# Attention outputs of two heads in one strip of a PSUM bank, and a phase's outputs turned by four transposes

## The reference

```python
x = x + L0_attn(layernorm(x))                # 16 heads of 8: causal, linear attention with elu + 1
x = x + L0_xattn(layernorm(x), ctx, mask)    # 16 heads of 8: 512 keys from ctx, masked softmax
x = x + L0_ffn(layernorm(x))                 # 8 experts, the best 2 of each token
x = x + L1_attn(layernorm(x))                # 16 heads of 8: 256 keys, a window of 128 back
x = x + L1_xattn(layernorm(x), ctx)          # 8 heads of 16: 512 keys, two softmaxes that share a sum,
                                             # then layernorm, relu ffn, layernorm
x = x + L1_ffn(layernorm(x))                 # ternary weights, gelu
# each softmax attention, per head:
attn = softmax(scores(q, k)); out = attn @ v
```

## Time and profile before

| | us |
|---|---|
| median of 3 runs | 1060.52 (1055.59 to 1060.76) |
| the profiled execution, whole | 1054.23 |
| its span, first to last instruction | 1052.5 |
| PE busy / weight loads busy | 848.7 / 475.7 |
| DVE / ACT / POOL busy | 666.6 / 488.6 / 321.2 |
| mean granted TensorE clock | 0.914 |

### The profile page before, as it was taken

How to read it: one execution, slowest core, us unless ns; L and a number is a source line. 1 busy time by engine, 2 the same in 40 slices (tenths; PEclk the granted TensorE clock), 3 DMA queues, 4 the chain that set the end, 5 groups by cost and what they waited for, 6 DMA issues and landing times.

```text
span 1052.5 us, 19620 instructions
## 1 busy us (share of the span) xinstructions
PE 848.7 (81%) x6455; PEld 475.7 (45%) x6522; DVE 666.6 (63%) x2234; ACT 488.6 (46%) x1017; POOL 321.2 (31%) x872
## 2 busy tenths in 40 slices
PE   0477786999999887989999877897999977866763
PEld 0344553443444543545555435674544444422452
DVE  6767556878777774777676757765678473533511
ACT  0432332655555553557666545365655625413331
POOL 6423333212132232224452224352421213320312
PEclk9788988999999998999999989799999998857875
DMA  6287876031230534345330447328140114233000
GB/s 193 60 157 158 179 175 132 20 54 30 42 69 5 107 92 84 71 81 106 52 83 26 66 89 155 54 95 127 34 71 4 48 21 84 74 64 63 2 6 5
DMA packets 124965, 79.85 MB, mean 76 GB/s; under 512 B 8312, under 2 KB 122176, under 8 KB 124736
## 3 DMA queue, kind: packets, MB, share of 16 engines
q1 hardware_dynamic: 124864, 78.59, 36.9%
HBM read 43.99 MB, written 32.90 MB: 73 GB/s over the span
## 4 chain that ended last, share of the span: by engine, by line
PE 45%; DVE 17%; DMA 13%; issue 7%; SPq 6%; POOL 6%; ACT 5%; DVEq 0%; another core or an unknown queue 0%; POOLq 0%; ACTq 0%
PE ob L1211 7%; PE mb L1153 6%; DMA cT<-ctxT_dram 5%; PE eb L1181 4%; PE side L1074 3%; PE eb L1182 3%; PE side L1082 3%; DMA bounce<-scratch 2%; DMA QW<-bounce 2%; PE side L1027 2%; DVE junk L1635 2%; PE side L1065 2%; PE side L1094 2%; DMA QP<-mrow 2%; DVE mx L1643 2%
## 5 line engine op out<-in xcount | busy, mean ns | idle before, releaser
L1365 ACT ACTIVATE probs<-eb 128x512 f32<-128x512 f32 (+1 forms) x512 | 274.8, 568 | 217.5 <-PE eb L1182 91.5
L1635 DVE CUSTOM_DVE_ANT_0 junk<-mb,maskq_add 128x512 bf16<-128x512 f32 x256 | 169.1, 688 | 49.0 <-PE mb L1153 37.4
L1211 PE MATMUL ob<-probs,V 128*32 128x256 f32 (+1 forms) x2048 | 133.3, 379 | 5.1 <-ACT probs L1365 2.2
L1643 DVE TENSOR_REDUCE mx<-mb 128x1 f32<-128x512 f32 x128 | 83.5, 685 | 56.1 <-PE mb L1153 53.7
L1181 PE MATMUL eb<-maskk_add,identb 128*128 128x512 bf16 x256 | 98.1, 383 | 9.7 <-issue 6.6
L964 POOL TENSOR_SCALAR nm<-mx 128x8 bf16<-128x8 f32 x80 | 20.1, 251 | 277.1 <-DVE mx L1635 117.9
L1153 PE MATMUL mb<-KS,QP 128*128 128x512 bf16 x227 | 81.3, 386 | 12.0 <-DVE mx L1635 6.9
L1182 PE MATMUL eb<-QP,KS 128*128 128x512 bf16 x231 | 88.3, 382 | 0.0
L1211 PEld LDWEIGHTS ob<-probs,V 128*32 128x32 f32 x2048 | 55.4, 111 | 65.6 <-issue 32.1
L874 POOL TENSOR_SCALAR rstd<-mv 128x2 f32<-128x2 f32 x64 | 16.5, 258 | 209.0 <-DVE mv L1431 207.8
L1374 ACT COPY OT<-ob 128x512 f32<-128x512 f32 x56 | 32.8, 585 | 73.4 <-PE ob L1205 44.0
(11 more groups left out here) (189 smaller groups left out, 1707.4 us busy)
## 6 DMA issues: line engine op xcount, KB each, us to landing
QP<-bounce SPq DMA_DIRECT2D x48, 256.0 KB, 5.5
KS<-bounce SPq DMA_DIRECT2D x32, 384.0 KB, 7.2
bounce<-scratch SPq DMA_DIRECT2D x48, 192.0 KB, 2.3
bounce<-scratch SPq DMA_DIRECT2D x64, 128.0 KB, 2.2
KS<-bounce SPq DMA_DIRECT2D x32, 192.0 KB, 6.0
bounce<-scratch SPq DMA_DIRECT2D x16, 384.0 KB, 2.6
cT<-ctxT_dram SPq DMA_DIRECT2D x16, 256.0 KB, 6.1
bounce<-scratch SPq DMA_DIRECT2D x16, 256.0 KB, 2.4
```

Of the source, the lines that this page charges most:

```text
L1211: ins = nc.tensor.matmul(bank[32 * j:32 * j + 32, S - n:S], v_of(core, kt, 4 * g + j), pr[:, (j % 2) * n:(j % 2 + 1) * n], start=(kt == 0) ...
L1365: nc.scalar.activation(probs[:, u % PROBS, 0:n], eb[:, u % 2, 0:n], ACT.Exp, scale=SCALE[core.p]).then_inc(probs_by[1], 1)
L1635: ins = V_.tensor_tensor_reduce(junk[:, e.n % 2, :], bank, maskq_add[:, t, :], 1.0, NEG_EXP, ALU.add, ALU.max, mx[slot][:, t, h:h + 1])
L1643: ins = V_.tensor_reduce(mx[slot][:, t, h:h + 1], bank, AX.X, ALU.max)
```

## The change

The values of heads 8 to 15 stand in columns 17 to 24 of their 32 and their 1.0 in column 25; heads 0 to 7 are as before. The group g + 2 adds its product onto the columns of group g in the same 256 columns of `ob`: only the first product of a strip clears, the last group ends the sum. All other columns of `V` are zero there, so the two heads don't mix. A phase now has one bank, one copy to `OT` (half as large as before) and one wait of the av; `outputs` turns all of `OT` by four 128x128 transposes and drops nothing, and `scaled` and `values` work on the lower and upper eight heads in an instruction each (two reciprocals and two products where one was). `v_of` also drops the tight packing of phase 3's values. In the planner `outputs` costs 0.65 instead of 1.8 (1.0 in phase 3), and a phase has one `keep`. Cut to its core:

```diff
@@ -40,7 +40,8 @@
-V_AT = (8, 8, 8, 0)
+
+V_AT = ((8, 17), (8, 17), (8, 17), (0,))
...
@@ -63,7 +64,7 @@
 
 
 def finish_steps(p):
-    return [("pe", "outputs", (1.8, 1.8, 1.8, 1.0)[p], ()), ("pool", "biased", 0.75, ()),
+    return [("pe", "outputs", 0.65, ()), ("pool", "biased", 0.75, ()),
             ("dve", "scaled", 0.95, ("outputs",)), ("pe", "scaled turned", 0.28, ("scaled",)), ("act", "scaled kept", 0.3, ("scaled turned",)),
             ("pe", "projected", 0.5, ("scaled kept",)), ("dve", "updated", 0.45, ("projected", "biased"))]
 
...
@@ -387,10 +387,9 @@
                 elif EXP_UNITS[core.p] * GROUPS[core.p] <= EARLY and exp_next == 1:
                     todo.append((CHAIN_OF[core.p + 1], core.b, t, core))
                 if u % QUAD == QUAD - 1:
-                    per = 2 * EXP_UNITS[core.p] // QUAD
                     a = Event("av", core, j // QUAD, 0, u // QUAD)
-                    a.first, a.last = a.g % per == 0, a.g % per == per - 1
-                    a.pair = sum(GROUPS[c.p] // 2 for c in exp_cores[:-1]) + a.g // per
+                    a.first, a.last = j == QUAD - 1, exp_next == EXP_UNITS[core.p] * GROUPS[core.p]
+                    a.turn = len(exp_cores) - 1
                     av_queue.append(a)
             elif kind == "exp":
                 ev = exp_queue.pop(0)
...
@@ -403,13 +402,12 @@
                 free[e] = t + AV_PE[ev.core.p]
                 av_done.append(free[e] + SEEN)
                 if ev.last:
-                    k = Event("keep", ev.core, ev.g // (2 * EXP_UNITS[ev.core.p] // QUAD), 0, ev.pair)
+                    k = Event("keep", ev.core, 0, 0, ev.turn)
                     k.made = free[e] + SEEN
                     keep_queue.append(k)
-                    if k.g == GROUPS[ev.core.p] // 2 - 1:
-                        slot_free[ev.core.slot] = free[e] + SEEN
-                        if ev.core.wide >= 0:
-                            wide_free[ev.core.wide] = free[e] + SEEN
+                    slot_free[ev.core.slot] = free[e] + SEEN
+                    if ev.core.wide >= 0:
+                        wide_free[ev.core.wide] = free[e] + SEEN
             elif kind == "keep":
                 ev = keep_queue.pop(0)
                 if ev.core.out < 0:
...
@@ -594,7 +590,7 @@
         nmr = sbs(SLOTS, "nmr", [P, TQ, 16])
         nm = sbs(SLOTS, "nm", [P, TQ, 16, PARTS], BF16)
         mrow = sbs(MROWS, "mrow", [MAX_ROWS, S], BF16)
-        OT = sbs(OUTS, "OT", [P, 4, S])
+        OT = sbs(OUTS, "OT", [P, 2, S])
         qn = sbs(QN, "qn", [P, TQ, D])
         cT = sbs(LANES, "cT", [P, SK])
 
...
@@ -972,7 +968,9 @@
                 for i in range(SLOTS):
                     yield 0.5 + 5 * i
                     link(G.memset(V[i][:], 0.0))
-                    G.memset(V[i][:, :, :, 16:17], 1.0).then_inc(values_init, 1)
+                    for j, at in enumerate(V_AT[0]):
+                        ins = G.memset(V[i][:, :, 8 * j:8 * j + 8, at + 8:at + 9], 1.0)
+                    ins.then_inc(values_init, 1)
 
             program("pool", {"nm": minus_maxima}, chain_steps, values())
 
...
@@ -1015,17 +1013,13 @@
             def finish(run, p):
                 l, o = run.lane, run.old.out
                 bank = side[:, l, :]
-                n, heads = HD[p] + 1, HEADS[p]
                 yield "outputs"
-                pe.wait_ge(out_kept, OB + PAIRS_TO[run.old])
+                pe.wait_ge(out_kept, OB + PHASES_TO[run.old])
                 if run.name in ("to1", "to3"):
                     pe.wait_ge(ctx_kept[l], N_CTX(run) + 1)
-                chosen = ident[:].rearrange("p (h e) -> p h e", e=VW)[:, :, V_AT[p]:V_AT[p] + n]
                 for t in range(TQ):
-                    for g in range(GROUPS[p]):
-                        lo = (t * heads + 4 * g) * n
-                        ins = nc.tensor.matmul(bank[:, lo:lo + 4 * n].rearrange("p (h e) -> p h e", e=n), OT[o][:, g, t * P:(t + 1) * P], chosen,
-                                               start=True, stop=True)
+                    for half in range(2):
+                        ins = nc.tensor.transpose(bank[:, (2 * t + half) * P:(2 * t + half + 1) * P], OT[o][:, half, t * P:(t + 1) * P], ident[:])
                 ins.then_inc(filled[l], 1)
                 yield "scaled turned"
                 pe.wait_ge(an_ready[l], N_FINISH(run) + 1)
...
@@ -1187,29 +1181,33 @@
 
             def values(core, g, i, u):
 
+
+
+
                 p = core.p
-                pair = PAIRS_TO[core] - GROUPS[p] // 2 + g // 2
-                bank = ob[:, pair % OB, (g % 2) * S:(g % 2 + 1) * S]
+                turn_ = PHASES_TO[core] - 1
+                bank = ob[:, turn_ % OB, (g % 2) * S:(g % 2 + 1) * S]
+                first_, end = g == 0, g >= GROUPS[p] - 2
                 pr = probs[:, u % PROBS, :]
                 kt = i // 2
                 heads = (2 * (i % 2), 2 * (i % 2) + 1)
-                if g % 2 == 0 and i == 0:
-                    pe.wait_ge(out_kept, pair + 1)
+                if g == 0 and i == 0:
+                    pe.wait_ge(out_kept, turn_ + 1)
                 if p == 0:
                     for t in range(TQ):
                         for j in heads:
                             at = ((j % 2) * TQ + t) * P
                             nc.tensor.matmul(bank[32 * j:32 * j + 32, t * P:(t + 1) * P], v_of(core, t, 4 * g + j), pr[:, at:at + P],
-                                             start=True, stop=(t == 0), skip_group_check=True)
+                                             start=(first_ and t == 0), stop=(end and t == 0), skip_group_check=True)
                     for j in heads:
                         ins = nc.tensor.matmul(bank[32 * j:32 * j + 32, P:2 * P], KV[core.slot][:, 4 * g + j, :], qf[core.slot][:],
-                                               start=False, stop=True, skip_group_check=True)
+                                               start=False, stop=end, skip_group_check=True)
                 else:
                     n = (S, P)[kt] if p == 2 else S
                     last = 1 if p == 2 else TK - 1
                     for j in heads:
                         ins = nc.tensor.matmul(bank[32 * j:32 * j + 32, S - n:S], v_of(core, kt, 4 * g + j), pr[:, (j % 2) * n:(j % 2 + 1) * n],
-                                               start=(kt == 0), stop=(kt == last), skip_group_check=True)
+                                               start=(first_ and kt == 0), stop=(end and kt == last), skip_group_check=True)
                 ins.then_inc(av_done, 1)
 
             def value_sums(e):
...
@@ -1366,12 +1364,11 @@
 
             def keep_outputs(e):
                 core = e.core
-                units = UNITS_TO[core] - (GROUPS[core.p] // 2 - 1 - e.g) * 2 * EXP_UNITS[core.p]
-                act.wait_ge(av_done, units)
+                act.wait_ge(av_done, UNITS_TO[core])
                 last = OLD_RUN[OUT_BEFORE[core]] if OUT_BEFORE[core] else None
                 if last:
                     act.wait_ge(filled[last.lane], fill(last, "outputs"))
-                nc.scalar.copy(OT[core.out][:, 2 * e.g:2 * e.g + 2, :].rearrange("p g q -> p (g q)"), ob[:, e.n % OB, :]).then_inc(out_kept, 1)
+                nc.scalar.copy(OT[core.out][:].rearrange("p g q -> p (g q)"), ob[:, e.n % OB, :]).then_inc(out_kept, 1)
 
             def prelude():
                 yield 18.0
...
@@ -1444,14 +1441,15 @@
                 dve.wait_ge(filled[l], fill(run, "v"))
                 dve.wait_ge(values_init, slot + 1)
                 slot_emptied(dve, run)
-                vb = side[:, l, 0:tk * D].rearrange("p (m d) -> p m d", d=hd)
-                dst = V[slot][:].rearrange("p t h e -> p (t h) e")[:, 0:tk * heads, V_AT[p]:V_AT[p] + hd]
-                if p == 3:
-                    ins = V_.tensor_copy(dst, vb)
-                else:
-                    bias = row(f"v{p}").rearrange("p (h d) -> p h d", d=hd)
-                    for t in range(tk):
-                        ins = V_.tensor_tensor(dst[:, t * heads:(t + 1) * heads, :], vb[:, t * heads:(t + 1) * heads, :], bias, ALU.add)
+                vb = side[:, l, 0:tk * D].rearrange("p (t h d) -> p t h d", t=tk, d=hd)
+                for j, at in enumerate(V_AT[p]):
+                    h = slice(8 * j, 8 * j + 8)
+                    dst = V[slot][:, 0:tk, h, at:at + hd]
+                    if p == 3:
+                        ins = V_.tensor_copy(dst, vb)
+                    else:
+                        bias = row(f"v{p}").rearrange("p (h d) -> p h d", d=hd)[:, h, :]
+                        ins = V_.tensor_tensor(dst, vb[:, :, h, :], bias.unsqueeze(1).to_broadcast([P, tk, 8, hd]), ALU.add)
                 if p:
                     ins.then_inc(lane_free[l], 1)
 
...
@@ -1488,18 +1486,24 @@
                 n = N_FINISH(run)
                 yield "scaled"
                 dve.wait_ge(filled[l], fill(run, "outputs"))
-                m = TQ * heads
```

(25 more changed lines are left out.)

## The result

| | us | ratio to the kernel before |
|---|---|---|
| before, median of 4 runs | 1060.46 (1055.59 to 1060.76) | |
| after, median of 4 runs | 1089.54 (1087.22 to 1090.27) | 1.0282 (1.0253 to 1.0310) |
| after, the profiled execution / its span | 1087.22 / 1085.4 | |

What follows compares the result with a forecast made beforehand. No engine is full over the span (PE highest, 81%); PE bounds the long phases, an image's own chain the last stretch. From 1057 us, -14 - 2 + 4 + 24 + 5 = +17 gave 1074 us, range 1042 to 1094.

Steps and rivals of the forecast that it cites:

- (3,5): Phase 3 of image 5, moved from behind (1,7) to ahead of (1,6): free before, now paid elsewhere, +24 us.
- The frame: Behind (1,6), image 6's chain still needs 81 us; (1,7) fills 41, the other 40 stay nearly empty.
- rival B: Faster: greedy order costs nothing, chains run earlier, last stretch shortens by what (3,5) cost; 1045 us, chance 0.20.
- Outputs: On PE, four transposes replace eight products per finish, 0.75 us instead of 1.86: -14 us (bounds -28 and -8).
- Copies: On ACT, 56 copies of 585 ns become 32, cutting waits on PE: -2 us (0 to -5.6).
- Scaling: On DVE, one more reciprocal and product per finish, 0.3 us at 32 finishes: +4 us (0 to +9.5).
- The three together: The terms for outputs, copies and scaling, -14, -2 and +4 us: -12 us.
- The base: Starting time of 1057 us for the forecast, the middle between the profiled execution and the median of the runs.
- The second order effect: Between (1,5) and (1,6), ten short phases in a row instead of seven: +5 us (-5 to +30).
- Rival D: Worse: the ten short phases starve PE and its clock falls; 1093 us (1085 to 1105), chance 0.13.

Runs made afterwards that it cites:

- e1: The changed kernel with the planner of the kernel before (old costs, a copy per pair): 1056.85 us, ratio 0.9934 to the kernel before.
- e5: The changed kernel with its own cost of 0.65, but the whole list of phases of the kernel before forced: 1039.53 us, ratio 0.9770.
- e12: The changed kernel with phase 3 of images 0 and 1 ahead of (1,5), (3,4) ahead of (2,5), (3,5) behind (1,7): 1041.37 us, ratio 0.9795.
- e10: The changed kernel at cost 0.60 with a list putting (3,4), (3,5) behind (1,7) and (0,6), (0,7) ahead of (3,3): 1027.32 us, ratio 0.9659.
- e11: The order of e10 with the old layout of the kernel before: 1037.98 us, ratio 0.9754.
- e4: The changed kernel with only phase 3 of image 5 moved back behind phase 1 of image 7: 1053.52 us, ratio 0.9897.
- e2: The kernel before, old layout, with the order that the changed planner makes: 1118.82 us, ratio 1.0516.
- e3: The changed kernel with only the planner's cost of the outputs set to 0.60 instead of 0.65: 1080.51 us, ratio 1.0161.
- e6: The changed kernel at its cost of 0.65, with the list of e3 forced, so only (0,7) moves ahead of (3,4): 1088.23 us, ratio 1.0236.
- e7: The changed kernel, its list held, with no lane for a to3 chain while no query buffer is free: 1086.63 us, ratio 1.0209.
- e8: The changed kernel, same list, with three instead of two buffers for the queries of phase 3: 1082.91 us, ratio 1.0188.
- e9: The kernel e5 with only phase 3 of image 5 moved from behind (1,7) to ahead of (1,6): 1095.94 us, ratio 1.0301.

## Why the prediction was wrong in its size

All kernels in one table. "Per phase" is the time from the last exponential of (1,5) to the first of (1,6), divided by the short phases between them; "(0,6) to (1,6)" goes from the last product with the triangle of (0,6) to the first exponential of (1,6). "(1,6) ends" is its last exponential, "chain" the time from there to the first of (2,6), "rest" the time from there to the end:

| | run of short phases | per phase | between (1,7) and (2,6) | (0,6) to (1,6) | (1,6) ends | chain | rest | ratio |
|---|---|---|---|---|---|---|---|---|
| before | 7 | 23.8 | (3,5) | 78 | 786.9 | 81 | 184 | 1 |
| e1 | 7 | 23.9 | (3,5) | 78 | 792.6 | 84 | 182 | 0.993 |
| e5 | 7 | 24.0 | (3,5) | 89 | 789.2 | 78 | 170 | 0.977 |
| e12 | 7 | 25.1 | (3,5) | 98 | 794.9 | 84 | 164 | 0.980 |
| e10 | 6 | 25.3 | (3,4), (3,5) | 90 | 760.3 | 79 | 182 | 0.966 |
| e11 (old layout) | 6 | 26.0 | (3,4), (3,5) | 95 | 776.6 | 80 | 183 | 0.975 |
| e4 | 9 | 28.5 | (3,5) | 69 | 810.4 | 81 | 164 | 0.990 |
| after | 10 | 26.7 | none | 72 | 831.2 | 77 | 178 | 1.028 |
| e2 (old layout) | 10 | 27.3 | none | 73 | 855.7 | 79 | 183 | 1.052 |
| e3 | 10 | 25.4 | none | 89 | 813.1 | 81 | 181 | 1.016 |
| e6 | 10 | 27.1 | none | 69 | 839.3 | 82 | 165 | 1.024 |
| e7 | 10 | 27.5 | none | 81 | 828.1 | 72 | 184 | 1.021 |
| e8 | 10 | 26.1 | none | 69 | 826.6 | 77 | 177 | 1.019 |
| e9 | 8 | 27.9 | none | 145 | 846.6 | 80 | 166 | 1.030 |

**The frame held.** Image 6's chain takes 77 to 84 us from (1,6), and 72 in e7, whether none, one or two phases stand in the gap behind (1,7). So what decides is first when (1,6) ends, and everything that stands ahead of it has its price. That was the argument on (3,5), and rival B, by which the gap would close, fell. The rest varies too, by 20 us, and not with what fills the gap.

**Outputs.** Right in kind. Four transposes end after 0.66 us, 0.75 was taken. The Trainium skill (TensorE: Matmul & The Clock Gate, "Part 4: PE-mode transpose") has some 275 ns for one, beside a figure for bf16. A single record here, of f32 data, is 284 ns in the mean, which is near it, but the four overlap (0.66 us for 4 x 0.284 = 1.14), so the time of one is not to be taken four times.

**Copies.** 32 of 584 ns, as said. What was waited for them didn't fall: PE and its loads waited 3.7 + 1.8 + 0.3 us for L1371, for 2.1 + 1.8 + 1.7 before. The -2 was about nothing, inside its bounds.

**Scaling.** 2 x 230 + 2 x 286 = 1032 ns for 354 + 424 = 778, 0.25 us more per finish, 0.3 taken. But phase 3, with its eight heads, keeps one instruction of each kind, so 24 finishes pay it and not the 32 of the sum. PE's wait for it behind `outputs` grew: 11.5 us for L1504 in front of L1027's products, for 3.3 in front of L1033. The row of after:

```profile
L1027 PE MATMUL side<-ident,An 128*128 128x128 f32 x64 | 14.0, 301 | 11.5 <-DVE An L1504 11.5
```

**The three together** were put at -12. They measured -7 (e1), -10 (e10 against e11), -24 where the planner was allowed to use the shorter finish in the same list of phases (e5), and -25 in the changed order (after against e2). So the layout was worth between half and twice what was forecast, depending on the order that it stands in. With the instructions in before's order, which is where the terms were read, 5 of the 12 did not come.

**The base.** 1057 was chosen between the profiled execution and the median; the medians stayed at 1060.5, which is 3.5 of the miss.

**(3,5).** Priced at +24. By the end of (1,7) it is 25.5 (e4), so the term was right where it was worked out. By the ratios the move was worth 41, and part of that is e4's last stretch, 14 us shorter. This can't be put down to the filled gap: the rest is as short in e6 and e9, which have nothing in the gap (165 and 166), and 182 to 184 in before, e1 and e10, which have it filled.

**The second order effect: this is the step that failed.** The prediction said of the three further short phases in the run: "I take **+5** (-5 to +30, the upper end if six or seven of the ten pay it)". The last exponential of (1,7) starts at 874.6 in after, the second of its row above. Here it is in e5 (the first of its row) and in e1 (the second, at 832.6):

```profile
830.71 1.09 ACT L1365 ACTIVATE probs<-eb 128x512 f32<-128x512 f32 x2
```

```profile
832.10 1.09 ACT L1368 ACTIVATE probs<-eb 128x512 f32<-128x512 f32 x2 [0.94 <-PE eb L1181]
```

Both kernels have the new layout and the old list of phases, e5 with the new cost in the planner, e1 with the old one. After reaches the end of (1,7) 44 and 42 us later. Take off the 24 that (3,5) was priced at, and 20 and 18 us remain where 5 were put. Over the whole program the order costs 54 us by the ratios against e5 and 37 against e1, so that 30 or 13 remain. What sets these apart from the 18 to 20 lies in the last stretches, which vary by 20 us among all kernels, and in the spread of the runs. So the term measured 13 to 30, and 18 to 20 in the part of the program that it was about; the price of a short phase was carried over from stretches with another mix, and the correction for it was too small.

It doesn't follow that the length of the run is the cause. Per phase the run of ten costs 26.7 us in after and 25.4 in e3, that of nine in e4 28.5, and that of six in e10 25.3, for 23.8 in before. Nor is it more waiting of PE: the waits that the trace names come to 24.9 us in the 167 us of before's run and 41.4 in the 265 of after's, that is 3.6 and 4.1 per phase, 6 us in ten phases. What they are for has changed, from DMA (19.2 us, then 13.0) to DVE (2.4, then 19.8). The largest two waits of PE in after from 520.4 to 785.6 (us in total, times, longest):

```profile
PE mb L1147 <- DVE mx L1647: 10.9, 15, 5.1
PE side L1088 <- DMA cT<-ctxT_dram: 7.1, 2, 5.4
```

and in before, from 577.2 to 744:

```profile
PE side L1094 <- DMA cT<-ctxT_dram: 8.8, 2, 5.3
PE mb L1153 <- DMA QW<-bounce: 8.4, 2, 6.3
```

The new wait is for the maxima of phase 3 (L1647): the run of ten has six phases 3, that of seven three. The larger part is busy time: 22.2 us of PE per phase in after's run for 20.2 in before's.

What else the traces show is image 6's own way to (1,6). In after, one more short phase, (2,5), stands ahead of (0,6), and (0,7) stands behind (3,4) and (3,5). (0,6) ends at 713.6, in before at 666.5. The first scores for the maxima of (1,6) then wait for the landing of image 6's stack, and in after those of (1,7) wait for image 7's. Rows on PE in before, then in after for both images:

```profile
720.46 0.38 PE L1153 MATMUL mb<-KS,QP 128*128 128x512 bf16 x1 [1.28 <-DMA KS<-bounce]
```

```profile
752.90 0.59 PE L1147 MATMUL mb<-KS,QP 128*128 128x512 bf16 x2 [0.72 <-DMA KS<-bounce]
822.93 1.01 PE L1147 MATMUL mb<-KS,QP 128*128 128x512 bf16 x2 [3.61 <-DMA KS<-bounce]
```

From (0,6) to (1,6) it takes 69 to 73 us in after, e2, e4, e6 and e8, which have (2,5) ahead of (0,6), and 78 to 98 in before, e1, e5, e10, e11 and e12, which have it behind; e7 with 81 and e3 with 89 have it ahead and are no shorter. So a late image 6, whose chain then has little room, is as good a reading of the 18 to 20 us as the length of the run. e8 fits it: its stop went, (0,6) ended no earlier, and little was gained. Against it: e4, e10 and e12 show no wait for that stack. No run moved (0,6) or (2,5) alone, so neither reading is shown.

**In sum:** forecast 1057 - 12 + 29 = 1074. Measured, by e1, 1060.5 - 7 + 37 = 1090, where the order missed by 8, the layout by 5 and the base by 3.5; by e5, 1060.5 - 24 + 54 = 1090, where two larger misses, 25 in the order and 12 in the layout, partly cancel. That 1089.5 lies inside the range owes something to this: the upper bound was kept wide for just this term.

**Rival D** (1093) has nearly the time, but not its mechanism: PE is not starved to the 68% and clock 0.75 that it was worked out with, the run has 84% at 0.92. A lower clock is seen as well, 0.895 over the span in after's profiled execution for 0.914 before, 0.923 in e5 and 0.912 in e10; the same 6202 records of PE take 852.3 us in after and 826.0 in e10. Whether that is a cause of the length or follows from it, no run here separates.

**Open.** What makes the phases between (1,5) and (1,6) dear: their number, the late image 6, or a resource. Held lane and third wide buffer were tried, each moved at most 10 us, and a fourth lane or slot was not tried. Why the last stretch takes 164 to 170 us in e4, e12, e6, e9 and e5 and 177 to 184 in the others. And why the layout is worth 24 and 25 us in two pairs of kernels and 7 to 10 in the others.

## What to carry over

When an edit changes the cost that a build-time planner works with, it is two changes: run the new code in the old order and the old code in the new order before judging either; here they were -7 and +55 us, and the good edit would have been dropped with the bad order. Where one chain sets the end, find the room in its shadow (here 33 us, empty in after) and keep work for it; moving one short phase into it brought 25 us ahead of it (e4), and the best order here has two in it (e10, where image 6 also came earlier). And a price per phase read from one mix of phases holds for that mix only: besides how many phases stand ahead of the last images, look at when those images' own chains start.

## What the runs showed that was not expected

Two kernels with the same list of phases and 0.05 us between their entries for one step differ by 8 us (e3, e6), and the layout in one list gains 7 or 24 us according to the planner's costs (e1, e5). The four transposes kept their advantage at the low clock: 1.10 us where the sixteen records took 3.41, a factor of 3.1, and 0.66 for 1.95, a factor of 3.0, at the high one.
